# Two attention blocks with expert layers: the exponential of a quad in three instructions, and the second block's normalisation moments and gathers in another order

## The chip, the cores and the metric

The kernel runs on one core of one Trainium2 chip. The metric is the device time of one execution in microseconds. Three runs of the kernel before gave 1275.87, 1277.16 and 1281.9 us, median 1277.16 us.

## What is computed

16 sequences of 112 tokens, model width 256, go through two layers. Each layer adds a cross attention and then a sparse feed-forward part to the residual x:

```
x = x + L0_xcond(layernorm(x), ctx, ctx, tau, delta)      # 16 heads of 16, 375 keys
x = x + L0_ffn(layernorm(x))                              # 64 experts, 8 chosen, and a shared one
x = x + L1_xcond(layernorm(x), ctx, ctx, tau, delta)
x = x + L1_ffn(layernorm(x))                              # 8 experts, 2 chosen

scores = einsum('blhe,bshe->bhls', q, k) * tau + delta
a      = softmax(scores / 4)
out    = einsum('bhls,bshd->blhd', a, v) @ Wo.T + bo
```

All of it is in float32.

## The kernel before, in words

Each engine has its own program, and semaphores couple them. Work falls into four stages: first attention, first experts, second attention, second experts. The change is in the attention stages (the function `attention(L)` of each engine), and what it does to the first attention and to the second differs.

**A batch and its steps.** The attention of a layer runs over 16 batches b (n counts them through both layers, so the second layer's are n = 16 to 31). A batch has NQ = 4 steps i, one for each quad of four heads. In a step TensorE (PE) does, in this order: `scores_T` (L671), the transposed scores of the quad, into PSUM banks 4 to 7, one bank a head, 3 x 112 = 336 columns each; `score_rows` (L653) of the quad that comes three steps later, into banks 0 to 3; the step's jobs; `pv` (L689), exponentials times values, into bank 0; and `max_T` (L661), the transpose of the row maxima. ScalarE (ACT) takes the exponential of banks 4 to 7 (`exp`, L1618) in two instructions of two banks each (672 columns), then evacuates the jobs' results, then `pv`'s (L1631) and `max_T`'s (L1625). VectorE (DVE) takes the row maxima in two instructions of two banks (`row_max`, L1073, "MAX"). `pv` waits for both exponentials and for the first maximum, `max_T` for the second.

**Jobs.** Tables written out by hand name for each step its jobs as (name, batch offset, bank): `FULL` for most batches, `SECOND_FULL` for batch 1 of the second layer, `OPENING_FULL` for batch 0, `CLOSING_FULL` for the last. Jobs are projections and transposes for neighbouring batches: OT and O2T (transposes of the attention output of the batch before, L604 and L585), OP (output projection, L590), XT (transpose of the normalised input of a later batch), Q, K0, K1, V0 to V2 (L590), XT2 and LG (for the router), RK (ranks of the chosen experts, L636). A job in banks 4 to 7 may only start when the exponential has read the bank: banks 4 and 5 wait for the first exponential of the step, 6 and 7 for the second (the line `prev = ...` in `body` of PE). Within a step PE executes in order, so a waiting job holds all that follows. `FIRST_JOBS` lists the work ahead of batch 0; its `FILL` entry issues that many matmuls whose result nobody reads.

**DVE.** `WORK` lists for each step what DVE does between and behind the two maxima. In the second layer: OT; C0 to C3, the sums of eight gathered expert rows into the residual of batch b+3 (`combine`, L1059); MOM, the moments of that residual (`moments`, L1048 and L1052), behind C2 and C3 in step 2 (so ahead of step 3's maxima); OP, MOM2 and LN2 (L1097), which add the attention output, take its moments and normalise it for the router of batch b-1; RK, SLOT, R0 to R3, W80 and W81, the routing. LN2 waits for the factor that POOL works out.

**POOL.** `body1` is the second layer's batch on GpSimd (POOL). In order: scatters of routed rows (L1943), `output_row_numbers` (L1949), gather 0; behind step 1's scores gathers 1 to 3 (L1957, an indirect DMA each) and `deviation(1)` (L1899, L1901), the factor that LN2 waits for; behind step 2's scores gathers 4 and 5, `copy_rows` (L1931, L1932) and `deviation(0)` of batch b+3, which waits for MOM; behind step 3's scores `apply` (L1913), the normalised input that job XT needs, gathers 6 and 7, `add_bias` (L1889). `first()` is the same ahead of batch 0: the gathers of batches 0 to 3, with `normalise(0, base + 2, 2)` between the fourth and the fifth gather of batch 3, then three `add_bias`.

**SyncE** moves queries, keys and transposed maxima in SBUF in its own order (`stream`); the change doesn't touch it, nor any DMA of ACT.

Of the kernel before, what the change touches and what calls it, by code (L numbers as in the profile page):

```python
# [17 lines left out]
ACT = mybir.ActivationFunctionType  # L18
# [3 lines left out]
B, Q, S, D = 16, 112, 375, 256  # L22
KD = D // P
NH, DH = 16, 16
ST, KT = 3, 125
TB = Q * B
EPS = 1e-5
QUAD = 4
NQ = NH // QUAD
# [59 lines left out]
def build(nc, a, acc):  # L89
# [12 lines left out]
    with ctx:  # L102
# [108 lines left out]
        act = sb("act", [P, EM])  # L211
# [117 lines left out]
        def quarters(i):  # L329
# [19 lines left out]
                (("K0", 2, 5), ("RK", -2, 4), ("XT2", -1, 6)),  # L349
                (("K1", 2, 4), ("LG", -1, 5)))  # L350
        OPENING_FULL = ((("K0", 2, 5),), (("Q", 2, 5),), (("K1", 2, 5),), ()), ((("K0", 2, 5),), (("K1", 2, 5),), (("XT", 2, 5),), (("Q", 2, 5),))
        SECOND_FULL = ((("OT", -1, 4), ("V2", 1, 5), ("V0", 1, 7)),
                       (("O2T", -1, 4), ("XT", 2, 5), ("OP", -1, 6), ("V1", 1, 7)),
                       (("K0", 2, 5), ("Q", 2, 4), ("XT2", -1, 6)),
# [11 lines left out]
        TABLE_BANK = 0, 3  # L366

# [32 lines left out]
        def in_layer(b, offset):  # L400

            return not isinstance(b, int) or 0 <= b + offset < B
# [175 lines left out]
        def _(pe):  # L578
# [14 lines left out]
            def attention(L):  # L593
# [81 lines left out]
                def pv(n, u, i, rows_ahead):  # L675

                    g = n * NQ + i
                    pe.wait_ge(s_exp, g * 2 + 2)
                    if rows_ahead:
                        pe.wait_ge(s_max, g * 2 + (2 * AHEAD + 1))  # L680
                    else:
                        pe.wait_ge(s_oev, g)
                    if i == 0:
                        for j in ("V0", "V1", "V2"):
                            pe.wait_ge(ev[j], n + 1)
                    for t in range(ST):
                        for j in range(QUAD):
                            h = QUAD * i + j
                            last = pe.matmul(bank[OUT_BANK][ROW * j:ROW * j + DV, 0:Q], vv[:, u, t, h * DV:(h + 1) * DV],  # L689
                                             pT[:, i % 2 * QUAD + j, t * Q:(t + 1) * Q], start=(t == 0), stop=(t == ST - 1), tile_position=(0, ROW * j))  # L690
                    last.then_inc(s_pv, 1)
# [43 lines left out]
                def body(n, b, u):  # L735
# [9 lines left out]
                    for i in range(NQ):  # L745
# [5 lines left out]
                        for j, r, k in jobs_of(l, b)[i]:  # L751
                            prev = closing.get(k, (s_max, n * (2 * NQ) + 2 * NQ)) if k < 4 else (s_exp, n * (2 * NQ) + (2 * i + (1 if k < 6 else 2)))
# [242 lines left out]
        def _(dve):  # L995
# [69 lines left out]
            def attention(L):  # L1065
# [131 lines left out]
                else:  # L1197
                    WORK = ((("OT", -1), ("MAX", 0), ("C0", 3), ("C1", 3)),
# [408 lines left out]
        def _(act):  # L1607
            def attention(L):
# [3 lines left out]
                def exp(n, i, p):  # L1612

                    g = n * NQ + i
                    act.wait_ge(s_st, g + 1)
                    wait(act, s_pv, g - 1)
                    slot, first_bank = i % 2 * QUAD + 2 * p, ROWS_T + 2 * p
                    act.activation(pT[:, slot:slot + 2, :], banks[0:KT, first_bank:first_bank + 2, 0:ST * Q], ACT.Exp, scale=0.25).then_inc(s_exp, 1)  # L1618
# [109 lines left out]
                def body(n, b, u):  # L1728
                    for i in range(NQ):
                        if i == 2 and (in_layer(b, 3) or l == 0):  # L1730
                            load_ctx((b + 3) % B, 1 - u)
                        exp(n, i, 0)
                        exp(n, i, 1)
# [145 lines left out]
        def _(pool):  # L1879
# [79 lines left out]
            def attention(L):  # L1959
# [3 lines left out]
                def first():  # L1963
                    if l:
# [10 lines left out]
                        gather(3, 1, 0, 4)  # L1975
                        normalise(0, base + 2, 2)
                        gather(3, 1, 4, 4)
# [37 lines left out]
                def body1(n, b):  # L2015
# [14 lines left out]
                    if in_layer(b, -1):  # L2030
                        copy_rows(L, n - 1, b - 1)
                    if in_layer(b, 3):
                        deviation(0, n + 3)
# [3 lines left out]
                    if in_layer(b, 4):  # L2037
                        gather(b + 4, b % 2, 6, 2)
# [161 lines left out]
```

## Time and profile before

| what | value |
|---|---|
| median of three runs | 1277.16 us |
| the profiled execution's own time | 1275.19 us |
| its span, first to last instruction | 1273.3 us |
| busy: PE, DVE, ACT, POOL | 93%, 66%, 40%, 42% |
| mean granted TensorE clock | 0.969 of full |
| first attention, first scores at | 35.07 us |
| second attention, from about 640 us to about | 992 us |

Busy shares are means over four stages with different limits. Start times below are microseconds from the first instruction. In a timeline a row can stand for several instructions of one kind that follow each other (x2 is two); what stands in square brackets is the idle time of the engine just ahead of it, and what ended that. The ends of matmuls are modelled, and consecutive ones overlap. Two instructions of one engine can overlap too: the two exponentials of 0.73 us stand in the timeline as x2 with 1.35 us.

### The profile page before, as it was taken

To read this page: it belongs to the slowest core of one execution; us is meant where nothing else is said; L and a number is where in the kernel's file an instruction comes from. 1 tells how busy PE (TensorE), PEld (TensorE's weight loads), DVE (VectorE), ACT (ScalarE), POOL (GpSimd) and SP (SyncE) were. 2 spreads that over 40 slices of the span, in tenths; PEclk is the share of its full clock that TensorE was granted. 3 is DMA by queue.
4 is the path that set the end of the run, shared out by engine and by line. 5 is a ranking of instruction groups with operands and counts; after the bars stand their busy time and mean duration, and the time that the engine had idled before them with its cause. 6 is when DMAs were issued, how large, how long until landed. Compare 5 with 4: busy or idle time off the path is not lost.

```text
span 1273.3 us, 38557 instructions
## 1 busy us (share of the span) xinstructions
PE 1178.8 (93%) x12856; PEld 929.5 (73%) x12857; DVE 836.6 (66%) x2657; ACT 512.0 (40%) x1289; POOL 535.7 (42%) x691
## 2 busy tenths in 40 slices
PE   6899999998888999999888999998998999999996
PEld 3566666666657999899545666666666899999995
DVE  3468888887876677666555788888875554444442
ACT  2455555555532444444134555555554122222221
POOL 2036666665572001100557667676622223222332
PEclk9899999999998999999977999999997999999998
DMA  4235454546536678865223333333315123353311
GB/s 127 91 126 169 153 167 141 176 148 194 157 102 206 196 217 260 264 179 174 85 80 96 91 110 100 105 103 106 93 49 210 47 39 107 103 168 107 104 33 29
DMA packets 115809, 165.79 MB, mean 130 GB/s; under 512 B 26448, under 2 KB 96736, under 8 KB 114640
## 3 DMA queue, kind: packets, MB, share of 16 engines
q0 software_dynamic: 22672, 58.41, 17.1%
q1 hardware_dynamic: 46464, 53.43, 13.9%
q10 hardware_dynamic: 46528, 52.06, 12.8%
q8 instruction: 86, 1.41, 0.5%
q14 instruction: 59, 0.48, 0.1%
HBM read 85.99 MB, written 61.66 MB: 116 GB/s over the span
## 4 chain that ended last, share of the span: by engine, by line
PE 49%; DVE 9%; issue 6%; POOL 5%; ACT 2%; DMA 1%; DVEq 0%; POOLq 0%; SPq 0%; ACTq 0%
PE banks L945 12%; PE banks L879 9%; PE banks L953 6%; PE banks L590 6%; PE banks L887 4%; PE banks L867 3%; PE banks L671 3%; POOL kept L1957 2%; PE banks L689 2%; DVE mx L1073 2%; DVE resid L1059 2%; ACT shared_buf L1618 1%; POOL xs_d L1943 1%; DVE st L1048 1%; PE banks L661 1%
## 5 line engine op out<-in xcount | busy, mean ns | idle before, releaser
L1073 DVE TENSOR_REDUCE mx<-banks 112x2 f32<-112x750 f32 x256 | 230.8, 933 | 82.3 <-PE banks L653 75.5
L1618 ACT ACTIVATE shared_buf<-banks 125x672 f32<-125x672 f32 x256 | 173.1, 728 | 90.3 <-PE banks L671 86.9
L1943 POOL DMA_INDIRECT xs_d<-xns,idx x160 | 154.3, 964 | 115.5 <-issue 50.2
L1957 POOL DMA_INDIRECT kept<-y_d,yidx x128 | 124.5, 973 | 100.8 <-issue 81.7
L945 PEld LDWEIGHTS banks<-xT,attn_buf 128*128 128x128 f32 x1364 | 157.1, 192 | 1.6
L945 PE MATMUL banks<-xT,attn_buf 128*128 128x128 f32 x1364 | 157.3, 275 | 0.0
L879 PE MATMUL banks<-xT,staged 128*128 128x128 f32 x1064 | 143.5, 278 | 4.6 <-DVE staged L1486 3.8
L879 PEld LDWEIGHTS banks<-xT,staged 128*128 128x128 f32 x1064 | 130.9, 194 | 7.8 <-issue 5.5
L2117 POOL DMA_INDIRECT out<-shared_buf,ids x31 | 53.7, 1733 | 170.1 <-ACT shared_buf L1845 125.9
L590 PE MATMUL banks<-attn_buf,wk 128*128 128x375 f32 x256 | 103.0, 526 | 23.8 <-ACT shared_buf L1618 13.1
L671 PE MATMUL banks<-attn_buf 18*125 18x112 f32 x3072 | 121.5, 288 | 1.1 <-issue 0.5
L671 PEld LDWEIGHTS banks<-attn_buf 18*125 18x125 f32 x3072 | 98.8, 188 | 27.9 <-issue 27.1
L653 PE MATMUL banks<-attn_buf 17*112 17x375 f32 x1024 | 110.1, 498 | 1.7 <-issue 1.7
L689 PE MATMUL banks<-shared_buf,vv 125*17 125x112 f32 x3072 | 102.1, 267 | 8.6 <-DVE mx L1073 8.4
L590 PEld LDWEIGHTS banks<-attn_buf,wk 128*128 128x128 f32 x256 | 45.9, 199 | 78.7 <-ACT shared_buf L1618 48.6
L590 PE MATMUL banks<-wv,attn_buf 128*125 128x256 f32 x384 | 101.9, 391 | 0.7 <-ACT qT L1654 0.7
L689 PEld LDWEIGHTS banks<-shared_buf,vv 125*17 125x17 f32 x3072 | 68.9, 99 | 39.7 <-issue 30.9
L953 PE MATMUL banks<-ringbuf,shared_buf 128*128 x372 | 85.4, 379 | 0.0
L1792 ACT ACTIVATE sgate<-banks 128x128 f32<-128x128 f32 x133 | 36.9, 278 | 113.8 <-PE banks L879 113.8
L1475 DVE COPY xT<-banks 128x256 f32<-128x256 f32 x166 | 70.1, 423 | 16.2 <-DVE yidx_all L1449 7.0
L887 PE MATMUL banks<-ringbuf,shared_buf 128*128 x264 | 79.3, 382 | 0.0
L590 PEld LDWEIGHTS banks<-wv,attn_buf 128*125 128x125 f32 x384 | 69.3, 193 | 12.7 <-issue 2.9
(221 smaller groups left out, 1902.9 us busy)
## 6 DMA issues: line engine op xcount, KB each, us to landing
shared_buf<-xs_d SPq DMA_DIRECT2D x136, 128.0 KB, 2.8
y_d<-shared_buf ACTq DMA_DIRECT2D x132, 128.0 KB, 2.8
ringbuf<-in_we SPq DMA_DIRECT2D x6, 2176.0 KB, 8.8
ringbuf<-in_we POOLq DMA_DIRECT2D x32, 384.0 KB, 4.7
attn_buf<-attn_buf SPq DMA_DIRECT2D x128, 93.8 KB
attn_buf<-in_ctxT ACTq DMA_DIRECT2D x29, 375.0 KB
y_d<-zrow ACTq DMA_DIRECT2D x16, 512.0 KB
xs_d<-zrow ACTq DMA_DIRECT2D x16, 512.0 KB
```

What stands on the lines that cost most here:

```text
L590: last = pe.matmul(dst, lhs(k), rhs(k), start=(k == 0), stop=(k == KD - 1))
L653: last = pe.matmul(bank[j][0:Q, 0:S], qT4[rows, u, i, :], kT4[rows, u, i, :], start=True, stop=True, tile_position=(ROW * j, 0))
L671: last = pe.matmul(bank[ROWS_T + j][0:KT, t * Q:(t + 1) * Q], kT4[rows, u, i, t * KT:(t + 1) * KT], qT4[rows, u, i, :], start=True, stop=T ...
L689: last = pe.matmul(bank[OUT_BANK][ROW * j:ROW * j + DV, 0:Q], vv[:, u, t, h * DV:(h + 1) * DV], pT[:, i % 2 * QUAD + j, t * Q:(t + 1) * Q] ...
L879: last = pe.matmul(bank[u % 2][:, j * P:(j + 1) * P], staged0[:, u % 2, (k * 2 + j) * P:(k * 2 + j + 1) * P], xT[:, u % 2, k, :], start=(k ...
L887: pe.matmul(bank[6 + u % 2][:, 0:D], hT[:, u % 2, 0:P], ringbuf[:, bass.ds(col + 2 * L.up, D)], start=True, stop=True).then_inc(s_dn[0], 1)
L945: last = pe.matmul(dst, weights[:, k * 2 * L.I + c * P:k * 2 * L.I + (c + 1) * P], xT[:, u % 2, k, :], start=(k == 0), stop=(k == KD - 1))
L953: last = pe.matmul(bank[7][:, 0:D], hT[:, u % 2, c * P:(c + 1) * P], ringbuf[:, bass.ds(col + 2 * L.up + c * D, D)], start=(c == 0), stop= ...
L1073: dve.tensor_reduce(mx[:, i % 2, 2 * p:2 * p + 2], banks[0:Q, 2 * p:2 * p + 2, 0:S], AX.X, ALU.max).then_inc(s_max, 1)
L1618: act.activation(pT[:, slot:slot + 2, :], banks[0:KT, first_bank:first_bank + 2, 0:ST * Q], ACT.Exp, scale=0.25).then_inc(s_exp, 1)
L1943: pool.indirect_dma_start(xs_d[L.number], bass.IndirectOffsetOnAxis(ap=idx[:, b % 2, k:k + 1], axis=0), rows, None).then_inc(s_scat[b % 2] ...
L1957: pool.indirect_dma_start(yg[:, u, k, :], None, y_d, bass.IndirectOffsetOnAxis(ap=yidx[:, u, k:k + 1], axis=0)).then_inc(s_gat[u][k * 4 // ...
```

## The change

The exponential of a quad is now taken in three instructions: bank 4 alone, bank 5 alone, banks 6 and 7 together. A job waits for as many of them as cover its bank. Where a step's first job was in bank 5 it is now in bank 4. In the second layer MOM goes from the end of step 2 to behind both maxima of step 3. POOL's gathers 6 and 7 go from behind `apply` to ahead of `deviation(0)`, and ahead of batch 0 all eight gathers of batch 3 go ahead of `normalise`. `FILL` in the second layer's `FIRST_JOBS` is 8 in place of 4.

```diff
-                      (("XT", 0, 0), ("Q", 0, 1), ("DOWN3", 0, 4), ("V2", 1, 4), ("BO", 0, 7), ("ROW0", 0, 0), ("V0", 1, 5), ("FILL", 4, 4), ("MAX0", 0, 6), ("ROW1", 0, 0),
+                      (("XT", 0, 0), ("Q", 0, 1), ("DOWN3", 0, 4), ("V2", 1, 4), ("BO", 0, 7), ("ROW0", 0, 0), ("V0", 1, 5), ("FILL", 8, 4), ("MAX0", 0, 6), ("ROW1", 0, 0),
...
         FULL = ((("OT", -1, 4), ("V2", 1, 5), ("XT", 2, 6), ("V0", 1, 7)),
                 (("O2T", -1, 4), ("Q", 2, 5), ("OP", -1, 6), ("V1", 1, 7)),
-                (("K0", 2, 5), ("RK", -2, 4), ("XT2", -1, 6)),
+                (("K0", 2, 4), ("RK", -2, 5), ("XT2", -1, 6)),
                 (("K1", 2, 4), ("LG", -1, 5)))
-        OPENING_FULL = ((("K0", 2, 5),), (("Q", 2, 5),), (("K1", 2, 5),), ()), ((("K0", 2, 5),), (("K1", 2, 5),), (("XT", 2, 5),), (("Q", 2, 5),))
+        OPENING_FULL = ((("K0", 2, 4),), (("Q", 2, 4),), (("K1", 2, 4),), ()), ((("K0", 2, 4),), (("K1", 2, 4),), (("XT", 2, 4),), (("Q", 2, 4),))
         SECOND_FULL = ((("OT", -1, 4), ("V2", 1, 5), ("V0", 1, 7)),
                        (("O2T", -1, 4), ("XT", 2, 5), ("OP", -1, 6), ("V1", 1, 7)),
-                       (("K0", 2, 5), ("Q", 2, 4), ("XT2", -1, 6)),
+                       (("K0", 2, 4), ("Q", 2, 5), ("XT2", -1, 6)),
                        (("K1", 2, 4), ("LG", -1, 5)))
...
+        EXP_BANKS = (0, 1), (1, 2), (2, QUAD)
+        EXPS = len(EXP_BANKS)
+
+        def exps_behind(k):
+
+            return next(p + 1 for p, (first, end) in enumerate(EXP_BANKS) if k - ROWS_T < end)
...
-                    pe.wait_ge(s_exp, g * 2 + 2)
+                    pe.wait_ge(s_exp, g * EXPS + EXPS)
...
-                            prev = closing.get(k, (s_max, n * (2 * NQ) + 2 * NQ)) if k < 4 else (s_exp, n * (2 * NQ) + (2 * i + (1 if k < 6 else 2)))
+                            prev = closing.get(k, (s_max, n * (2 * NQ) + 2 * NQ)) if k < 4 else (s_exp, n * (EXPS * NQ) + (EXPS * i + exps_behind(k)))
...
-                            (("MAX", 0), ("RK", -2), ("C2", 3), ("C3", 3), ("MOM", 3)),
-                            (("MAX", 0), ("SLOT", -2), ("R3", -2), ("W80", -2), ("W81", -2), ("R0", -1)))
+                            (("MAX", 0), ("RK", -2), ("C2", 3), ("C3", 3)),
+                            (("MAX", 0), ("MOM", 3), ("SLOT", -2), ("R3", -2), ("W80", -2), ("W81", -2), ("R0", -1)))
...
-                    slot, first_bank = i % 2 * QUAD + 2 * p, ROWS_T + 2 * p
-                    act.activation(pT[:, slot:slot + 2, :], banks[0:KT, first_bank:first_bank + 2, 0:ST * Q], ACT.Exp, scale=0.25).then_inc(s_exp, 1)
+                    first, end = EXP_BANKS[p]
+                    slot = i % 2 * QUAD
+                    act.activation(pT[:, slot + first:slot + end, :], banks[0:KT, ROWS_T + first:ROWS_T + end, 0:ST * Q], ACT.Exp, scale=0.25).then_inc(s_exp, 1)
...
-                        exp(n, i, 0)
-                        exp(n, i, 1)
+                        for p in range(EXPS):
+                            exp(n, i, p)
...
-                        gather(3, 1, 0, 4)
+                        gather(3, 1)
                         normalise(0, base + 2, 2)
-                        gather(3, 1, 4, 4)
...
+                    if in_layer(b, 4):
+                        gather(b + 4, b % 2, 6, 2)
                     if in_layer(b, 3):
                         deviation(0, n + 3)
                     after_scores(n, 3)
                     if in_layer(b, 3):
                         apply(0, n + 3, b + 3)
-                    if in_layer(b, 4):
-                        gather(b + 4, b % 2, 6, 2)
```

## Rows read from the trace of the kernel before

**Rows 1.** Windows, one batch of each attention: window, its length, busy us and count by engine, clock, DMA.
```profile
113.39:133.36 19.97, 19.11 (x283) 13.47 (x283) 16.83 (x68) 11.05 (x28) 13.34 (x17) 1.00 0.53 166
...
764.34:785.22 20.88, 19.28 (x284) 13.44 (x283) 17.15 (x49) 11.22 (x29) 14.65 (x21) 1.00 0.35 101
```

**Rows 2.** Waits by engine and line: us in total, times, longest.
```profile
PE banks L590 <- ACT shared_buf L1618: 13.5, 55, 1.7
...
PE banks L604 <- ACT shared_buf L1618: 10.9, 28, 0.8
```

**Rows 3.** Timeline, first attention, steps 0 and 1 of batch 4: start, us, engine, line, what.
```profile
116.97 0.93 DVE L1073 TENSOR_REDUCE mx<-banks 112x2 f32<-112x750 f32 x1
...
118.26 0.36 PE L661 MATMUL banks<-con,mx 112*4 112x112 f32 x2
...
119.54 1.35 ACT L1618 ACTIVATE shared_buf<-banks 125x672 f32<-125x672 f32 x2 [0.63 <-PE banks L671]
...
120.28 1.78 DVE L1073 TENSOR_REDUCE mx<-banks 112x2 f32<-112x750 f32 x2 [0.30 <-PE banks L653]
...
120.32 0.41 PE L585 MATMUL banks<-con,o 112*128 112x112 f32 x2 [0.22 <-ACT shared_buf L1618]
...
120.78 0.36 ACT L1644 ACTIVATE o2T<-banks 128x224 f32<-128x224 f32 x1
...
122.53 0.42 DVE L1089 TENSOR_TENSOR resid<-banks,resid 112x256 f32<-112x256 f32 x1 [0.47 <-PE banks L590]
```

**Rows 4.** Groups by line and form, ACT: busy us, mean ns of one, idle before.
```profile
L1618 ACT ACTIVATE shared_buf<-banks 125x672 f32<-125x672 f32 x256 | 173.1, 728 | 90.3 <-PE banks L671 86.9 <-issue 3.4
...
L1665 ACT ACTIVATE vv<-banks 125x256 f32<-125x256 f32 x96 | 37.0, 385 | 88.3 <-PE banks L590 87.2 <-issue 1.0
```

**Rows 5.** Timeline, DVE, second attention, batches 19 to 21.
```profile
747.92 2.14 DVE L1059 SCALAR_TENSOR_TENSOR resid<-kept,w,resid 112x256 f32<-112x256 f32 x4
...
756.41 0.41 DVE L1097 TENSOR_SCALAR xn<-resid,mv,rstd 112x256 f32<-112x256 f32 x1 [0.62 <-POOL rstd L1901]
...
758.98 2.35 DVE L1059 SCALAR_TENSOR_TENSOR resid<-kept,w,resid 112x256 f32<-112x256 f32 x4
...
762.07 0.18 DVE L1052 BATCH_NORM_AGGREGATE mv<-st 112x2 f32<-112x6 f32 x1 [0.17 <-DVE st L1048]
762.21 1.78 DVE L1073 TENSOR_REDUCE mx<-banks 112x2 f32<-112x750 f32 x2
...
777.27 0.41 DVE L1097 TENSOR_SCALAR xn<-resid,mv,rstd 112x256 f32<-112x256 f32 x1 [0.61 <-POOL rstd L1901]
```

**Rows 6.** Timeline, POOL, second attention, batches 19 and 20.
```profile
762.44 0.21 POOL L1899 TENSOR_SCALAR veps<-mv 112x1 f32<-112x1 f32 x1 [2.66 <-DVE mv L1052]
...
763.43 1.24 POOL L1913 TENSOR_SCALAR xn<-resid,mv,rstd 112x256 f32<-112x256 f32 x1
...
767.18 0.73 POOL L1889 TENSOR_TENSOR resid<-resid,bo 112x256 f32<-112x256 f32 x1
```

**Rows 7.** Timeline, POOL, DVE and PE, opening of the second attention, to batch 17.
```profile
662.12 0.23 POOL L1899 TENSOR_SCALAR veps<-mv 112x1 f32<-112x1 f32 x1 [8.83 <-DVE mv L1052]
...
669.52 2.10 POOL L1889 TENSOR_TENSOR resid<-resid,bo 112x256 f32<-112x256 f32 x3
...
692.33 0.41 DVE L1097 TENSOR_SCALAR xn<-resid,mv,rstd 112x256 f32<-112x256 f32 x1 [7.28 <-POOL rstd L1901]
...
692.88 0.60 PE L585 MATMUL banks<-con,xn 112*128 112x112 f32 x2 [3.38 <-DVE xn L1097]
```

**Rows 8.** Windows of the opening (columns as in rows 1; the clock is third from the end).
```profile
640.00:675.00 35.00, 30.38 (x312) 17.86 (x310) 20.70 (x35) 13.21 (x29) 20.05 (x25) 0.66 0.30 83
675.00:705.00 30.00, 24.73 (x304) 16.69 (x297) 15.75 (x29) 12.70 (x29) 22.56 (x30) 0.83 0.36 99
```

**Rows 9.** Timeline, PE, where the opening's filling matmuls stand.
```profile
639.12 1.05 PE L696 MATMUL banks<-con 128*128 128x128 f32 x8
641.29 0.35 PE L661 MATMUL banks<-con,mx 112*4 112x112 f32 x2 [1.11 <-DVE mx L1073]
```

## The prediction

> **What bounds the kernel now.** Only the two attention stages are touched, so I first took the windows of one batch in each [rows 1]. In the first attention a batch lasts 19.97 us and PE is busy for 19.11 of it, in the second 20.88 with 19.28 busy. PE leads, but the second stage's batch is 0.9 longer for the same PE work, so there another loop sets the pace. Next the waits by line [rows 2]: PE waits for the exponential in nearly every step, 83 times in two rows alone, 24.4 us together. The timeline of a step shows that wait [rows 3]: the exponentials start at 119.54, the first is over 0.73 later, the step's first job starts at 120.32 behind 0.22 us of idle. DVE has little air either. In the same batch its only waits for PE are 0.30 (rows of scores) and 0.47 (OP), so its own chain needs 19.97 - 0.77 = 19.2 us a batch.
>
> In the second attention DVE waits 0.62 for POOL's factor ahead of LN2 [rows 5], and POOL waits 2.66 for DVE's moments [rows 6]. This closes a loop. From LN2's start at 756.41 to the end of MOM at 762.25 is 5.84 us, from there to the next LN2 at 777.27 is 15.02, together 20.86: the batch's 20.88. **This loop, not PE, sets the second attention's batch.** Last the opening: in batch 17 LN2 waits 7.28 and PE 3.38 for it [rows 7], and the clock stands at 0.66 and 0.83 of full in its two windows [rows 8].
>
> **Three exponentials.** No row has 336 columns. ACT's two nearest forms are 256 columns at 385 ns and 672 at 728 [rows 4], 0.82 ns a column, so I take 0.45 us (bounds 0.385 and 0.57, halfway to the larger form). Two exponentials overlap by 2 x 0.73 - 1.35 = 0.11, so three end after 0.45 + 0.45 + 0.73 - 0.22 = 1.41 in place of 1.35. Bank 4 is free 0.28 earlier, bank 5 0.07 later, banks 6 and 7 0.06 later. Every step's first job is now in bank 4 and is longer than the 0.34 until the next bank comes (the shortest, L585, shows 0.41), so the later banks wait for nobody. ACT's 128 extra instructions add 8 us to an engine 40% busy; what they delay is the evacuation queued behind them. That bites once: O2T's evacuation begins when the exponentials end (120.78) and OP needs it, so step 1 gains about 0.1 instead of what the others gain, 0.22 to 0.28 (I take 0.27). On PE alone that makes 3 x 0.27 + 0.1 = 0.9 a batch.
>
> In the first attention DVE doesn't give all of it. The tight cycle is OP, then DVE's chain to the second maximum of the next step 0, then `max_T`, then OP. That maximum ends at 117.90 and `max_T` starts at 118.26 [rows 3]; with some 0.15 for the hand-over 0.2 of slack is left. The cycle shortens by that and by step 1's 0.1: 0.3 a batch, 19.65. Over 14 batches 4.3, with the first and last batch 5.5. Bounds: 2 where the slack is less, and 14 (0.9 x 16) where DVE yields. I stay near the low one, as DVE's own 19.2 stands in the rows.
>
> **MOM behind the maxima, gathers ahead of `deviation(0)`** (second attention). The loop from LN2 to MOM now holds step 3's two maxima, 1.78 [rows 5]: 5.84 + 1.78 = 7.6. From MOM to LN2 two gathers leave POOL's path: `apply` ends at 764.67, `add_bias` starts at 767.18, so 2.51 less a 0.17 hand-over, 2.3. What is left is 12.7. The new period is 20.3, 0.57 less. The gathers go where POOL waited 2.66 [rows 6]; their 2.5 us end about when MOM ended before, and MOM now ends 1.8 later, so they are hidden with 1.5 to spare. Behind MOM wait only DVE's small routing steps (same total, same end) and POOL's `apply`, whose user, XT, comes late in the next step 0 and may wait 0.1 to 0.2 us, ahead of a wait of PE for DVE of about that size. PE's own loop of 20.88 - 1.6 (its idle) - 0.2 and DVE's of 17.15 busy plus gaps stay below 20.3. Batches 19 to 27 hold all of this: 9 x 0.57 = 5.1. Batches 18 and 28 to 31 have fewer gathers and lean on PE; I give them 2.0 together, and batches 16 and 17 0.5 from the exponentials. The bounds of this part are 2 and 12 (0.9 x 14).
>
> **All gathers of batch 3 ahead of `normalise`.** POOL waited 8.83 us at 662.12 for the moments, and the four gathers take 5.0 (two took 2.51 above), so they fit inside. `add_bias`, at 669.52 before [rows 7], starts 5.0 earlier and with it everything up to the factor for batch 17's LN2: that comes about 5 us earlier, against a wait of PE of 3.38. So the whole wait goes; next late is nothing, as K0 and Q occupy PE until about then. The clock follows. The mean of 0.83 over 30 us is 10.2 us at 1.2 GHz [rows 8], behind a gap of 3.38; about 2 of them are the gap's end, the other 8 cost half, 4. Together 7.3. Bounds: 4.0, if the clock falls all the same, and 8.
>
> **FILL 8.** Eight matmul instructions, four of FILL's, take 1.05 us and are followed by 1.11 us of idle [rows 9]; four more fill just that gap, cost 0 (0.1 if they overrun). Over the 35 us from 640 on the clock averaged 0.66, which is 24 us at the lower level [rows 8], and this gap is the first in them. With it filled I expect the clock to hold for about the first half of those 24. That spares at most half of 12 us, of which DVE's sums behind step 0's maxima take back a third: 4. Bounds 0 and 6; the second half has a gap of its own (DVE's moments between two maxima of batch 16), which stays.
>
> **Sum**, against the profiled execution's 1275.2: 5.5 + 5.1 + 2.0 + 0.5 + 7.3 + 4 = 24.4, so 1250.8. The median of the runs shown is 2.0 above that execution; I give half of it, **1252 us**.
>
> **Rivals.** (A) *The clock falls as before in the opening*, FILL or not: then 4 of the 24 are lost, 1256; and if it falls in batch 17 too, 1260. For: the clock doesn't follow the sum of the gaps, since a batch of the second attention has 1.6 us of idle and keeps 1.00 [rows 1]. Against: the largest gap ahead of each is removed.
>
> (B) *PE's 0.9 comes through in full*: DVE's chain in the first attention packs tighter once the rows come earlier. 1252 - 8.5 = 1243. For: DVE is busy for only 16.83 of 19.97 us. Against: the rest is hand-overs inside dependent chains, which no earlier row shortens.
>
> (C) *POOL and DVE block one another.* Four sums of DVE with two SBUF inputs take 2.14 us in step 0 and 2.35 beside POOL's copies [rows 5]. MOM's move puts POOL's `apply`, 1.24 us, beside DVE's two-input routing steps instead of beside the maxima, which read PSUM. If one held the other for its whole length the loop would be 20.3 + 1.24 = 21.5, 0.66 above the 20.88 of before: 5.9 lost in place of 5.1 gained, 1263. The Trainium skill's page "SBUF — State Buffer", section "Who interferes with whom", states this rule: two SBUF inputs on VectorE and a GpSimd instruction that reads SBUF exclude each other for a whole instruction. The trace agrees only that something of the kind exists and prices it at 0.2 for four sums, not 1.24.
>
> (D) *Slower*: PE's many short waits become one. In the new loop PE runs ahead and meets DVE at step 0's `max_T`, with a wait of 0.8 to 1.3 us in each of the batches 19 to 27. If that makes the clock fall as the opening's gap of 1.11 did, each batch runs partly at 1.2 GHz: PE's 19 us with 10 at half is +5, less the 1.3 of idle it eats, so about 3.7 over the 20.3, and 9 x 3.7 = 33, less the 24: 1284. It decides from three batches in four on. Against: the batch in rows 1 keeps 1.00 with 1.6 us of idle in all.
>
> (E) *The earlier bank frees nobody*, because the weight load ahead of the job costs what the wait cost: 5.5 + 2.5 less, 1260.
>
> **Chances.** My forecast 0.43, A 0.20, B 0.13, C 0.06, E 0.11, D 0.03, 0.04 for something unforeseen near no change. The range takes in B with the FILL bound and A and E together: 1242 to 1264. Half a percent, 6.4 us, is about what a measurement of this kernel can tell from no change: faster 0.93, within it 0.04, slower 0.03.
>
> **What the profile after would show.** Right: three exponentials in about 1.41, the first job of a step with no wait for ACT; first-attention batches of 19.6 to 19.7 with DVE's waits for PE shrunk; second-attention batches of 20.3 with POOL's wait for DVE's moments about 1.5; batch 17 without the gap of 3.4 and at full clock; the clock of 640 to 660 at 1.00. Wrong: a wait of PE for L1618 of still 0.2, a LN2 wait in batch 17 above 3 us, or new falls of the clock in batches 19 to 27.

## The result and the profile after

| | before | after |
|---|---|---|
| median of four runs each, same chip | 1277.91 us | 1261.22 us (1254.16 to 1264.85) |
| profiled execution | 1275.19 us | 1254.16 us |
| its span | 1273.3 us | 1252.3 us |
| first attention, from the first scores of batch 0 to those of batch 15's last step | 316.27 | 312.30 |
| second attention, the same | 338.71 | 323.27 |
| the rest of the span | 618.3 | 616.7 |
| time at 1.2 GHz, up to 1240 us | 71.7 | 41.0 |

The ratio is 0.9868, 95% interval 0.984 to 0.9897: 16.7 us faster, with 1252 forecast and a range of 1242 to 1264. The profiled execution of after is the fastest of its four: its mean granted clock is 0.980, that of the others 0.971 to 0.974. So the trace shows 21 us of gain where the medians show 16.7. Here and below a median is over all runs of a kernel, while a ratio leaves out the few that were more than 1.5% slower than the kernel's fastest.

Of the trace's 21 us, 15.4 came in the second attention, 4.0 in the first and 1.6 outside. The windows of the changed kernel: two batches of the first attention, one of the second (from LN2 to LN2), and the opening's two windows (columns as in rows 1).
```profile
149.70:169.31 19.61, 19.26 (x283) 13.49 (x282) 16.86 (x66) 11.41 (x32) 13.32 (x17) 1.00 0.51 155
129.55:149.70 20.15, 19.36 (x283) 13.53 (x283) 16.86 (x66) 11.40 (x32) 13.31 (x17) 1.00 0.52 163
801.00:821.45 20.45, 19.70 (x284) 13.37 (x283) 17.23 (x48) 11.68 (x33) 14.78 (x21) 1.00 0.44 111
640.00:675.00 35.00, 30.11 (x377) 18.59 (x375) 23.59 (x40) 17.37 (x43) 26.30 (x33) 0.80 0.43 108
675.00:705.00 30.00, 29.81 (x427) 20.92 (x427) 22.69 (x51) 16.97 (x48) 22.57 (x31) 1.00 0.41 108
```
In the first attention there are now two kinds of batch, 19.61 and 20.15 us. The 19.97 of [rows 1] was one of the shortest before: batches 2 to 11, where the clock stands at full in both kernels, took 19.97 to 20.44 us, 20.20 in the mean, and take 19.88 now. The second attention's is 20.45 in place of 20.88. Between 675 and 705 us PE is busy for 29.81 of 30 us at full clock, where [rows 8] had 24.73 at 0.83.

The three exponentials stand as foreseen (timeline, first attention, step 2): 1.42 us together, and the job starts 0.50 after their start, with no idle time of PE ahead of it, where [rows 3] had 0.78 and 0.22 of idle.
```profile
302.39 1.42 ACT L1625 ACTIVATE shared_buf<-banks 125x336 f32<-125x336 f32 x3 [0.63 <-PE banks L677]
...
302.89 1.22 PE L596 MATMUL banks<-attn_buf,wk 128*128 128x375 f32 x3
```
Where the gain stands shows in the lengths of a batch's four steps, from `scores_T` to `scores_T`: 5.16, 5.61, 4.75 and 4.45 us before (batch 4), 5.14, 5.55, 4.75 and 4.17 after (batch 6). Only step 3 keeps its 0.28. In step 0 `max_T` now starts 0.84 behind `pv` in place of 0.59, since DVE's second maximum isn't there, and in step 2 the gain is lost ahead of the next `scores_T` (0.28 of idle). From OP to the next step 0's `max_T` it is 16.51 us in place of 16.76, from there to OP 3.10 in place of 3.21.

**The first attention lost one wait and found another.** PE's waits between 34 and 380 us (us in total, times, longest), first before:
```profile
PE banks L590 <- ACT shared_buf L1618: 7.7, 28, 1.7
PE banks L604 <- ACT shared_buf L1618: 5.2, 14, 0.8
...
PE banks L585 <- ACT shared_buf L1618: 1.7, 8, 0.2
...
PE banks L653 <- issue: 1.0, 5, 0.3
```
and after (L659 is `score_rows`, L677 `scores_T`, L596 the projections; L1625 the exponential):
```profile
PE banks L659 <- issue: 5.1, 9, 1.0
PE banks L677 <- issue: 3.3, 11, 0.5
...
PE banks L667 <- DVE mx L1079: 1.9, 4, 0.9
...
PE banks L596 <- ACT shared_buf L1625: 1.4, 1, 1.4
```
13.2 of the 14.6 us of waiting for the exponential went; 4.1 came back ahead of `score_rows`, and 2.8 ahead of `scores_T` (0.5 before, for L671). What `score_rows` waits for shows in SyncE's issues, here at the ends of batches 4 and 5, with PE's rows of scores of step 1 of batches 5 and 6, the first that need these keys (timeline, queue of SyncE, and PE):
```profile
128.36 3.80 SPq L447 DMA_DIRECT2D attn_buf<-qT  x4
132.28 1.18 SPq L442 DMA_DIRECT2D attn_buf<-attn_buf  x2
...
136.11 0.90 PE L659 MATMUL banks<-attn_buf 17*112 17x375 f32 x8 [0.50 <-issue]
...
148.51 2.49 SPq L447 DMA_DIRECT2D attn_buf<-qT  x4
151.11 1.27 SPq L442 DMA_DIRECT2D attn_buf<-attn_buf  x2
...
155.58 0.81 PE L659 MATMUL banks<-attn_buf 17*112 17x375 f32 x8
```
The second half of a batch's key rows (L442) stands on SyncE behind four query rows (L447). Ahead of 6 of the batches 1 to 14 these take 2.5 to 2.9 us to issue; ahead of the other 8 one of the four takes 1.5 to 1.95 in place of 0.6, and the key rows come 1.0 to 1.3 later. Ahead of batches 5 to 11 the query rows took 3.80, 2.49, 3.79, 3.84, 2.49, 2.49 and 3.50 us to issue, and these batches 20.15, 19.61, 20.13, 20.16, 19.61, 19.61 and 20.15: one to one. The earlier four don't follow it all the way (3.80, 3.68, 2.50 and 3.55 go with 19.64, 19.70, 19.69 and 19.96), and batches 12 to 14 are longer in part for other reasons (20.92, 20.44, 21.23). Firmer is the distance: in 8 of the 9 batches with this wait the rows of scores start 2.5 to 2.7 us behind the end of the key rows' issue; in batches without it they start 2.7 to 3.4 behind. The same slow issue stood in the kernel before (timeline, queue of SyncE). There the rows of scores came later and met it by 0.15 to 0.25 us only, five times, also 2.6 to 2.7 us behind the issue:
```profile
131.90 3.79 SPq L441 DMA_DIRECT2D attn_buf<-qT  x4
135.80 1.18 SPq L436 DMA_DIRECT2D attn_buf<-attn_buf  x2
```

**The second attention's loop** (timeline, DVE, POOL and PE):
```profile
801.00 0.41 DVE L1103 TENSOR_SCALAR xn<-resid,mv,rstd 112x256 f32<-112x256 f32 x1
...
808.48 0.22 POOL L1906 TENSOR_SCALAR veps<-mv 112x1 f32<-112x1 f32 x1 [1.58 <-DVE mv L1058]
...
813.57 0.35 PE L667 MATMUL banks<-con,mx 112*4 112x112 f32 x2 [0.65 <-DVE mx L1079]
...
821.45 0.41 DVE L1103 TENSOR_SCALAR xn<-resid,mv,rstd 112x256 f32<-112x256 f32 x1 [0.44 <-POOL rstd L1908]
```
From LN2 to POOL's start behind MOM are 7.5 us, from there to the next LN2 13.0: LN2 still waits for POOL and POOL for MOM, so the same loop still closes, 0.4 shorter. In each of the batches 19 to 26, before and after, LN2 starts 0.25 to 0.27 behind the end of POOL's factor, and POOL waits for MOM, 2.66 before and about 1.57 after. PE's four waits of 0.22 for the exponential and one of 0.74 ahead of step 3's `pv` have become one of 0.65 at `max_T`.

**The last batch of the second attention** gave 3.0 of the 15.4 us, and they go with the clock (windows over the first three steps of batch 31, before and after, columns as in rows 1):
```profile
970.37:988.92 18.55, 16.97 (x186) 12.31 (x185) 7.67 (x35) 5.85 (x14) 3.76 (x7) 0.54 0.87 331
952.37:967.89 15.52, 12.51 (x185) 9.02 (x185) 7.30 (x32) 6.03 (x17) 3.76 (x7) 0.78 0.92 356
```
17.1 us of it were at 1.2 GHz before, 6.8 after.

### The profile page after: what moved, and what is told of

It reads as the page before. It is cut to its first block, busy times and chain, and to the rows that moved or that the text cites. A ratio compares the mean times of both kernels' runs of the same rounds, so it can differ in the third digit from the quotient of the medians.

```text
span 1252.3 us, 38827 instructions
## 1 busy us (share of the span) xinstructions
PE 1172.1 (94%) x12864; PEld 923.9 (74%) x12865; DVE 836.8 (67%) x2657; ACT 521.8 (42%) x1417; POOL 537.6 (43%) x691
## 3 DMA queue, kind: packets, MB, share of 16 engines
q8 instruction: 86, 1.41, 0.5%
## 4 chain that ended last, share of the span: by engine, by line
PE 49%; DVE 14%; issue 7%; POOL 2%; ACT 1%; DMA 1%; DVEq 1%; POOLq 0%; ACTq 0%
PE banks L951 13%; PE banks L885 10%; PE banks L959 6%; PE banks L596 6%; DVE mx L1079 4%; PE banks L893 4%; PE banks L873 3%; PE banks L677 2%; DVE resid L1065 2%; PE banks L659 2%; PE banks L695 1%; POOL kept L1964 1%; DVE st L1054 1%; PE banks L667 1%; DVE eq L1128 1%
## 5 line engine op out<-in xcount | busy, mean ns | idle before, releaser
L1625 ACT ACTIVATE shared_buf<-banks 125x336 f32<-125x336 f32 (+1 forms) x384 | 181.1, 544 | 86.9 <-PE banks L677 83.0
L677 PE MATMUL banks<-attn_buf 18*125 18x112 f32 x3072 | 119.4, 285 | 4.2 <-issue 4.0
L677 PEld LDWEIGHTS banks<-attn_buf 18*125 18x125 f32 x3072 | 97.1, 185 | 30.8 <-issue 30.2
L659 PE MATMUL banks<-attn_buf 17*112 17x375 f32 x1024 | 107.6, 486 | 7.4 <-issue 6.8
L596 PE MATMUL banks<-attn_buf,wk 128*128 128x375 f32 x256 | 100.4, 515 | 10.9 <-DMA wv<-in_wv 9.2
L596 PE MATMUL banks<-wv,attn_buf 128*125 128x256 f32 x384 | 101.1, 389 | 1.3 <-ACT qT L1661 0.7
L596 PEld LDWEIGHTS banks<-attn_buf,wk 128*128 128x128 f32 x256 | 44.7, 194 | 60.6 <-ACT shared_buf L1625 29.5
L1572 DVE TENSOR_TENSOR shared_buf<-sgate,banks 128x512 f32<-128x512 f32 x32 | 22.0, 687 | 85.8 <-ACT sgate L1843 85.8
```

The lines of the kernel that those rows point to most:

```text
L596: last = pe.matmul(dst, lhs(k), rhs(k), start=(k == 0), stop=(k == KD - 1))
L659: last = pe.matmul(bank[j][0:Q, 0:S], qT4[rows, u, i, :], kT4[rows, u, i, :], start=True, stop=True, tile_position=(ROW * j, 0))
L677: last = pe.matmul(bank[ROWS_T + j][0:KT, t * Q:(t + 1) * Q], kT4[rows, u, i, t * KT:(t + 1) * KT], qT4[rows, u, i, :], start=True, stop=T ...
L1625: act.activation(pT[:, slot + first:slot + end, :], banks[0:KT, ROWS_T + first:ROWS_T + end, 0:ST * Q], ACT.Exp, scale=0.25).then_inc(s_ex ...
```

## The experiments

Three groups, each with runs of the kernel before between its own. The first group, on one chip: 34 runs of before, median 1277.46 us, and 11 or 12 of each part of the change. Lengths of batches are of one profiled execution each.

**The three exponentials alone**, with the banks of the jobs:
```diff
+        EXP_BANKS = (0, 1), (1, 2), (2, QUAD)
...
-                (("K0", 2, 5), ("RK", -2, 4), ("XT2", -1, 6)),
+                (("K0", 2, 4), ("RK", -2, 5), ("XT2", -1, 6)),
```


> The three exponentials and the bank numbers alone, all else as before. Theory of loops: the first attention gets 4 us shorter, the second attention's batches 19 to 27 stay at 20.88 because DVE and POOL set them, so 5 to 8 us in all (1270 to 1273). Rival, every wait of PE that is removed comes off the time: 0.22 to 0.28 us in each of 103 steps, 23 to 29 us (1250 to 1255).

1274.79 us, ratio 0.9986 (0.9959 to 1.0012): not to be told from no change, and short of the 5 to 8 us expected. The second attention's batches 19 to 25 stay at 20.65 to 20.91, so that loop doesn't feel the exponentials, and the large gain of the rival is out. Batch 31 does differ: its first three steps take 15.5 us with 6.8 of them at 1.2 GHz, as in the whole change, where before and the three other parts have 16.8 to 18.6 us with 13 to 17. That is one execution each, and why is open. PE's waits in the first attention:
```profile
PE banks L659 <- issue: 5.7, 9, 1.0
PE banks L677 <- issue: 3.0, 10, 0.5
```
The new waits come with this part alone. One of them, 1.03 us at 217.01, stands at the start of a stretch with the clock at 0.57 (window, columns as in rows 1), which the kernel before doesn't have there. That the wait brought the fall isn't shown, as a wait of 0.96 in batch 1 had none behind it:
```profile
217.00:225.00 8.00, 7.99 (x56) 5.51 (x56) 3.69 (x11) 2.10 (x6) 3.56 (x6) 0.57 0.65 207
```

**The order alone** (MOM behind the maxima, gathers ahead of `deviation(0)`):
```diff
-                            (("MAX", 0), ("RK", -2), ("C2", 3), ("C3", 3), ("MOM", 3)),
-                            (("MAX", 0), ("SLOT", -2), ("R3", -2), ("W80", -2), ("W81", -2), ("R0", -1)))
+                            (("MAX", 0), ("RK", -2), ("C2", 3), ("C3", 3)),
+                            (("MAX", 0), ("MOM", 3), ("SLOT", -2), ("R3", -2), ("W80", -2), ("W81", -2), ("R0", -1)))
...
+                    if in_layer(b, 4):
+                        gather(b + 4, b % 2, 6, 2)
                     if in_layer(b, 3):
                         deviation(0, n + 3)
...
-                    if in_layer(b, 4):
-                        gather(b + 4, b % 2, 6, 2)
```


> MOM behind both maxima and gathers 6 and 7 ahead of deviation(0), nothing else. Theory of loops: batches 19 to 27 fall from 20.88 to about 20.35, 5 to 7 us in all (1271 to 1273). Rival, POOL and DVE exclude each other for whole instructions: these batches rise to 21.5, 6 us slower.

1275.02 us, ratio 0.9971 (0.9941 to 1.0001): the time alone tells little, and the 5 to 7 us expected didn't come. Batches 20 to 25 take 20.35 to 20.57 us, without the exponentials and with smaller waits of PE at `max_T`, 0.3 to 0.5 a batch (waits of 770 to 890 us):
```profile
POOL veps L1899 <- DVE mv L1052: 9.4, 6, 1.6
...
PE banks L661 <- DVE mx L1073: 1.9, 5, 0.5
```
LN2 again starts 0.25 to 0.28 behind POOL's factor. So it is the loop through LN2, MOM and POOL that makes the 20.4, not PE's wait of 0.65 in the whole change; and the batches are far from the 21.5 of rival C. What MOM's move and the gathers' move give each wasn't run.

**The gathers of the opening alone**, and **FILL 8 alone**:
```diff
-                        gather(3, 1, 0, 4)
+                        gather(3, 1)
                         normalise(0, base + 2, 2)
-                        gather(3, 1, 4, 4)
```


> Only batch 3's eight gathers ahead of normalise, before batch 0 of the second attention. Theory: the gap of 3.4 us in batch 17 goes and the fall of the clock behind it, batch 17 from 28.1 to about 21, 6 to 8 us in all (1270 to 1272). Rival, the clock falls somewhere else instead: 3.5 us.

1270.03 us, ratio 0.9953 (0.9924 to 0.9983), as expected.
```diff
-                      (("XT", 0, 0), ("Q", 0, 1), ("DOWN3", 0, 4), ("V2", 1, 4), ("BO", 0, 7), ("ROW0", 0, 0), ("V0", 1, 5), ("FILL", 4, 4), ("MAX0", 0, 6), ("ROW1", 0, 0),
+                      (("XT", 0, 0), ("Q", 0, 1), ("DOWN3", 0, 4), ("V2", 1, 4), ("BO", 0, 7), ("ROW0", 0, 0), ("V0", 1, 5), ("FILL", 8, 4), ("MAX0", 0, 6), ("ROW1", 0, 0),
```


> Only FILL 8 in place of 4. Theory of the prediction: the clock holds for the first half of the opening, 4 us (1274). Rival, where the clock falls depends on more than this gap, and it falls a few us later all the same: 0 to 2 us, which a measurement can't tell from none.

1273.3 us, ratio 0.9973 (0.9947 to 0.9999), near the 4 us expected. The opening's windows, with the gathers moved:
```profile
640.00:675.00 35.00, 30.36 (x278) 18.02 (x279) 20.04 (x34) 12.17 (x26) 23.46 (x29) 0.68 0.32 92
675.00:705.00 30.00, 28.53 (x374) 20.16 (x377) 20.75 (x39) 14.43 (x37) 21.43 (x28) 0.86 0.35 97
```
and with FILL 8:
```profile
640.00:675.00 35.00, 28.89 (x318) 18.73 (x320) 23.31 (x41) 12.92 (x29) 22.47 (x29) 0.89 0.34 96
675.00:705.00 30.00, 26.61 (x295) 18.17 (x288) 16.30 (x31) 11.67 (x28) 23.13 (x30) 0.73 0.34 93
```
The gathers take batch 17 from 28.13 to 22.93 us: the gap goes, and the clock doesn't fall at 691 us any more, but it stays low from 666 to 684 (17.1 us, where before had 10.2). FILL takes batch 16 from 24.12 to 21.37 and batch 17 from 28.13 to 29.18. In the whole change they take 22.59 and 19.91: together 9.8 us less than before, where the two edits alone add up to 6.9.

**What belongs to the clock.** The four medians are 2.7, 2.4, 7.4 and 4.2 us below before, together 16.7, the whole change's gain. That they meet is partly chance: by the means the four are together 12.7 below. The runs of one kernel spread by nine to twenty us, and with the mean granted clock. Over the 81 runs of this group, within each kernel, 0.01 of mean clock goes with 7.4 us (standard error 0.4), and only 1.7 us of scatter is left. With that slope the mean of each part splits:

| part | mean clock (before 0.969) | mean against before | of it with the clock | at equal clock |
|---|---|---|---|---|
| exponentials | 0.962 | -1.4 | +5.5 | -6.9 |
| order | 0.967 | -2.2 | +2.0 | -4.1 |
| opening's gathers | 0.972 | -6.2 | -2.0 | -4.2 |
| FILL 8 | 0.973 | -2.9 | -2.5 | -0.4 |

The last column has a standard error of 0.6. It is a regression over runs, not an edit that holds the clock still; but it fits the traces: FILL works through the clock alone, and the exponentials give back in clock most of what they gain. Where they lose it is seen in one execution only: 20.5 us at 1.2 GHz in the first attention, where before had 6.8, and so has the whole change.

The second group, on another chip where the same kernel takes 8.5% longer (17 runs of before, median 1386.29 us, and 6 of each kernel, 12 of the third). First the change again, and without its FILL:

> The changed kernel once more, to see how far its time moves from execution to execution and with what. If the clock's falls are what differs: the batches keep their 19.6 to 20.5 us, and the time follows the number of us at 1.2 GHz (each about half a us), 1254 to 1265.

1370.58 us, ratio 0.9889 (0.982 to 0.9957). The range expected was the first chip's.

> The changed kernel with FILL 4, as before. Theory of the prediction, the filling keeps the clock up ahead of batch 0: 4 us slower than the changed kernel. Rival, the other parts have moved the falls anyway: within 1 us of it.

1364.62 us, ratio 0.9883 (0.9822 to 0.9945). Within the whole change FILL makes no difference that these runs can tell. Then MOM between the two maxima of step 3:
```diff
-                            (("MAX", 0), ("MOM", 3), ("SLOT", -2), ("R3", -2), ("W80", -2), ("W81", -2), ("R0", -1)))
+                            (("MOM", 3), ("MAX", 0), ("SLOT", -2), ("R3", -2), ("W80", -2), ("W81", -2), ("R0", -1)))
```


> The changed kernel with MOM between the two maxima of step 3 instead of behind both. Theory of the loop of DVE and POOL: 0.93 us less in the loop, so batches 19 to 27 fall from 20.42 to where the cycle through OP and max_T holds them, 19.9 to 20.0, 4 us in all. Rival, the wait of PE for the second maximum in step 0 (0.65 us) is what sets the batch, not the loop: no change, or slower by the 0.8 that the second maximum of step 3 comes later.

1368.83 us, ratio 0.991 (0.9875 to 0.9945): the same as the change. And delta loaded by ACT behind the last exponential of step 3, not by SyncE:
```diff
-                        load_delta((b + 2) % B, u)
...
                         for p in range(EXPS):
                             exp(n, i, p)
+                        if i == NQ - 1 and (in_layer(b, 2) or l == 0):
+                            act.dma_start(kT4[ONE:P:ROW, u].rearrange("p i s -> p (i s)"), a["delta"][bass.ds((b + 2) % B, 1), :].rearrange("o s -> (o s)").partition_broadcast(QUAD)).then_inc(s_delta[u], 16)
```


> The changed kernel with the load of the additive row issued by ACT behind the exponentials of step 3 instead of by SP ahead of the key rows. Theory: in the first attention PE's new stop ahead of step 1's score rows is the wait for the key rows' transfer, queued on SP; with 0.6 us less in that queue step 1 is 5.55 us in every batch instead of 6.1 in half of them, 3 us in all. Rival, the stop comes from something else: no change.

1367.73 us, ratio 0.9898 (0.9843 to 0.9953): no difference either. But neither of the last two got a real test, as the traces show: on this chip other waits set the batches. The exponentials, DVE's maxima and the evacuations stand, mostly 1.7 to 3 us at a time, for something that the trace calls remote, which is to say that it found no releaser on this core, though the matmuls that they read have ended by the record (changed kernel on this chip: waits over the span, and one in the timeline, 1.8 us behind the end of `pv`):
```profile
DVE mx L1079 <- remote: 50.0, 19, 11.4
...
ACT shared_buf L1625 <- remote: 25.0, 8, 8.4
```
```profile
831.92 0.77 PE L695 MATMUL banks<-shared_buf,vv 125*17 125x112 f32 x24
...
834.48 0.26 ACT L1638 ACTIVATE oT<-banks 128x112 f32<-128x112 f32 x1 [2.07 <-remote]
```
The first chip's traces have no such wait. Here the first attention's batches take 21.4 us and more from batch 4 on, the second's 21.7 to 25.7 between batches 18 and 27, and the wait ahead of step 1's rows of scores appears twice in place of nine times. What the remote wait is stays open.

The third group asks for the share of the exponentials in the whole and for a version that beats the change. It ran on a third chip, which behaves like the second (11 runs of before, median 1393.37 us, and 6 of each kernel). The second kernel is the change with two exponentials a quad and the banks of before.

> The changed kernel as it is, as the measure for the next three. Clock theory (the profiled execution of the change was a lucky one): the median is 15 to 18 us below before, and the profiled execution lies within 5 us of its own median. In the first attention the batches come in two kinds, 19.6 us and 20.1 us, and the longer kind is the one whose step 1 waits 0.3 to 0.5 us ahead of its rows of scores. Rival (the 20.1 are chance or clock): the two kinds don't go with that wait.

1370.65 us, ratio 0.9803 (0.9747 to 0.9858). Both numbers of the clock theory missed: the median is 22.7 us below before, and the profiled execution, at 1386.06 with a clock of 0.923, lies 15.4 above it.

> The whole change without its first part: two exponentials a quad and the banks of before; order, opening gathers and FILL 8 as in the change. Theory (the first part is worth 0.2 to 0.3 us a batch in the first attention and nothing in the second, whose batch is set by DVE and POOL): 3 us slower than the change, first attention 316 us from first to last batch in place of 312, second attention's batches 20.4 as with the change. Rival 1 (the exponentials carry more once the loop is looser): 7 to 10 us slower, second attention's batches 20.7 or more. Rival 2 (worth nothing): within 1 us of the change.

1374.65 us, ratio 0.9879 (0.984 to 0.9918).

> The change, with the load of delta issued by ACT behind the last exponential of step 3 and not by SP ahead of the key rows. Theory (in the changed kernel step 1's rows of scores wait for the key rows' transfer, which stands on SP's queue behind delta, 0.51 us, and the query rows): the key rows are issued 0.5 us earlier, the wait of 0.3 to 0.5 us in step 1 goes, the first attention's 20.1 us batches become 19.6, which with 8 such batches is 4 us. Rival (DVE's chain takes over at once): the wait goes but step 2 or step 0 grows by as much, 0 to 1 us.

1370.33 us, ratio 0.982 (0.977 to 0.9871). The fourth adds to it, in the second attention:
```diff
-                    WORK = ((("OT", -1), ("MAX", 0), ("C0", 3), ("C1", 3)),
+                    WORK = ((("MAX", 0), ("OT", -1), ("C0", 3), ("C1", 3)),
...
-                            (("MAX", 0), ("MOM", 3), ("SLOT", -2), ("R3", -2), ("W80", -2), ("W81", -2), ("R0", -1)))
+                            (("MOM", 3), ("MAX", 0), ("SLOT", -2), ("R3", -2), ("W80", -2), ("W81", -2), ("R0", -1)))
```


> The change, delta by ACT, and in the second attention DVE takes MOM between the two maxima behind step 3, and OT behind the second maximum behind step 0. Theory (the second attention's loop runs over LN2, MOM and POOL, and PE's only long wait there is 0.65 us at the first row of maxima of step 0): MOM 0.9 us earlier, so batches of 19 to 27 at 19.9 to 20.1 in place of 20.4, 3 to 4 us, and with delta's 4 us 7 us faster than the change. Rival (MOM in between makes step 3's second maximum 0.6 late, which takes the place of what it gave): batches stay at 20.4, no faster than c3.

1363.61 us, ratio 0.9784 (0.9732 to 0.9836).

What the exponentials are worth within the whole stays unsettled. The medians say 4.0 us, the ratios, 0.9803 against 0.9879, 10.6, and the split by clock (here 9.7 us for 0.01) 5.1 with a standard error of 2.3: more than nothing, but neither the theory's 3 nor the rival's 7 to 10 is excluded. Delta by ACT is again nothing that can be told. The last kernel has the lowest time of the group, 7.0 below the change by the medians, 2.6 by the ratios and 4.0 at equal clock (standard error 2.3). Its interval overlaps the change's, so it is a candidate and not a faster kernel. None of the expected batch lengths could be read: the profiled change has batches of 21.4 us and longer in the first attention from batch 4 on, and 22.4 to 27.9 for batches 18 to 29.

## Why the prediction was right, and where not

**The size is right, and it is no sum of right terms.** The predicted 24.4 us against the profiled execution meets 21.0 in the profile and 16.7 in the medians. By place, from the two traces:

| term | predicted | in the trace |
|---|---|---|
| first attention | 5.5 | 4.0 |
| batches 16 and 17 (exponentials, gathers, FILL) | 0.5 + 7.3 + 4 | 9.8 |
| batches 19 to 27 | 5.1 | 1.5 |
| batches 18 and 28 to 31 | 2.0 | 4.1 |
| all else | 0 | 1.6 |

In the last row but one 3.0 us are batch 31 and the clock, which no term foresaw: luck. And the fast profiled execution flatters the 1252: the median is 9 us above it.

**Exponentials: the mechanism right, SyncE and the clock left out.** 1.41 us for three is 1.42, PE's wait is gone, and a clean first-attention batch takes 19.61 us for 19.65 predicted. The tight cycle gave what it was said to give: 0.25 from OP to `max_T` for a slack of 0.2, 0.11 from there to OP for 0.1. Over batches 2 to 11 the mean fell by 0.32 for 0.3. At equal clock the part is worth 6.9 us for 5.5 and 0.5 predicted. The step that failed is that its price was named in durations only: tighter batches ran into the key rows (4.1 us of waits more than before), and alone the mean clock was 0.007 lower, 5.5 us. Of the change's steps I followed those of PE, ACT and DVE, and never asked whether SyncE's transfers would be there when PE came 0.3 earlier.

**Rival E is out**, as the earlier bank did free PE; so is B, 0.9 a batch: PE's busy time in a batch rose from 19.11 to 19.26 and the 19.61 leave no more. D's wait at `max_T` appeared as its mechanism said, but smaller, 0.65 in place of 0.8 to 1.3: eight times between 705 and 860 us, 5.4 us together, and no stretch at 1.2 GHz lies between 668 and 878 us. In batch 27 the clock did fall, below; the prediction had named that as a sign of being wrong.

**The order: 20.3 predicted, 20.42 measured, and then two bad batches.** The loop's halves were 7.6 and 12.7, and are 7.5 and 13.0. POOL's wait for MOM of 1.5 is 1.58. But the term of 5.1 for batches 19 to 27 came to 1.5: 3.4 from batches 19 to 25, and 1.9 lost in 26 and 27. There, POOL and DVE (timeline, changed kernel), with PE:
```profile
856.07 0.95 POOL L1950 DMA_INDIRECT xs_d<-xns,idx  x1 [2.13 <-issue]
...
864.01 0.41 DVE L1103 TENSOR_SCALAR xn<-resid,mv,rstd 112x256 f32<-112x256 f32 x1 [1.90 <-POOL rstd L1908]
...
864.57 0.38 PE L591 MATMUL banks<-con,xn 112*128 112x112 f32 x2 [0.86 <-DVE xn L1103]
865.42 0.77 PE L695 MATMUL banks<-shared_buf,vv 125*17 125x112 f32 x24 [0.46 <-DVE mx L1079]
875.96 0.77 PE L695 MATMUL banks<-shared_buf,vv 125*17 125x112 f32 x24 [0.83 <-issue]
877.38 0.35 PE L667 MATMUL banks<-con,mx 112*4 112x112 f32 x2 [0.65 <-DVE mx L1079]
```
In batch 26 the second scatter is held back 2.13 us where 0.30 is usual, and the batch is 1.65 longer than its neighbours. The same scatter of the kernel before (timeline, POOL) was held back 0.94:
```profile
874.43 0.94 POOL L1943 DMA_INDIRECT xs_d<-xns,idx  x1 [0.94 <-issue]
```
0.64 more than usual, and that batch was 0.62 longer: in both kernels a stall of POOL lengthens the batch by nearly its own length, which is the best sign that POOL is in the loop. With the order alone it is 2.13 too, with 21.81 and 23.08 us for the two batches. At the start of batch 27 something else follows (timeline, DVE and POOL, changed kernel; above a usual batch, below this one):
```profile
810.62 0.23 DVE L1176 TENSOR_SCALAR sc<-logits,wsum 112x8 f32<-112x8 f32 x1
810.89 0.73 POOL L1896 TENSOR_TENSOR resid<-resid,bo 112x256 f32<-112x256 f32 x1 [0.18 <-POOL xn L1920]
...
873.90 0.76 DVE L1176 TENSOR_SCALAR sc<-logits,wsum 112x8 f32<-112x8 f32 x1
873.90 0.72 POOL L1896 TENSOR_TENSOR resid<-resid,bo 112x256 f32<-112x256 f32 x1 [0.18 <-POOL xn L1920]
```
A routing step of DVE starts together with POOL's `add_bias` and lasts as long as it, 0.76 for 0.23. Another, beside `apply`, takes 0.41 for 0.23. With the order alone both are there too, 0.76 and 0.42. Counted from POOL's start behind MOM, DVE's first maximum of step 0 comes 0.79 later than in the usual batch, and PE's waits of 0.83 and 0.65 stand behind it. The clock falls from 879 to 882, which makes batch 27 22.18 us. The prediction took a steady loop; why the new order makes the scatter's stall longer stays open. The 2.0 for batches 18 and 28 to 31 came to 1.1 in batch 18, nothing in 28 to 30 and the 3.0 of the clock in batch 31.

**The opening's gathers: 7.3 predicted, 7.4 by the medians, 6.2 by the means.** The 8.83 of waiting did hold the four gathers; the factor comes in time for PE, and LN2's wait for it went from 7.28 to 2.87. In the whole change batches 16 and 17 went from 52.25 to 42.50 us, 9.8 less. The clock part, 4 by the prediction, came in the profile of the whole change (0.83 to 1.00) and only in small part with this edit alone (0.86).

**FILL: the mechanism right, its size within the whole not settled.** The 1.11 of idle at `max_T` is 0.22. The clock in 640 to 675 is 0.80 for 0.66, not the 1.00 that I named for the first 20 us; it falls from 646, behind the next waits (timeline, PE, changed kernel):
```profile
637.18 0.35 PE L667 MATMUL banks<-con,mx 112*4 112x112 f32 x2 [0.22 <-DVE mx L1079]
...
643.77 0.35 PE L667 MATMUL banks<-con,mx 112*4 112x112 f32 x2 [1.05 <-DVE mx L1079]
...
655.68 0.35 PE L667 MATMUL banks<-con,mx 112*4 112x112 f32 x2 [1.77 <-DVE mx L1079]
```
Between 640 and 660 it is 0.84. Alone FILL gave 4.2 by the medians (2.9 by the means) for 4 predicted; taken out of the whole on another chip it cost nothing that could be seen.

**Rival A** is half true: in the profiled execution batches 16 and 17 have 13.7 us at 1.2 GHz in place of 27.6, and the whole 41.0 in place of 71.7; in the other three runs the mean clock shows more of it, 0.006 to 0.009, which by the slope above is 4 to 7 us, most of the distance from the profiled 1254 to the median 1261. **Rival C is out as a price on every batch**: they are at 20.4 and not at 21.5, POOL's `apply` beside DVE's routing steps takes 1.24 us as it did beside the maxima [rows 6], and DVE is busy for 17.23 us in the batch where it was for 17.15. The rule on shared access (the Trainium skill, "SBUF — State Buffer", "Who interferes with whom") fits the trace in part: the two-input routing step that runs beside `apply` (L1128) takes 0.33 for 0.23 and doesn't wait for `apply`'s end 0.7 later, while in batch 27 a step of DVE was held for the whole length of POOL's `add_bias`.

## What to carry to other kernels

Where an edit lets one engine run ahead, list every producer that it will meet next, the DMA queue of an idle-looking engine too, and look for its slowest instance in the trace, not its usual one: a stall that is hidden today is the next wait. In a loop of dependent engines a stall of one engine comes through nearly whole, 0.64 as 0.62 before and 1.83 as 1.65 after, so a period read from the usual batch is a lower bound. And where runs spread with the granted clock, time each part over many runs and set the clock against the time, since a part can gain 7 us at equal clock and show 1.

## What the runs showed of the hardware that was not expected

The mean granted clock goes with most of the spread of one kernel on one chip: 34 runs of the kernel before lie between 1269.06 us (clock 0.978) and 1284.54, correlation -0.92. One part of the change shifted this mean by itself, from 0.969 to 0.962 with the exponentials.

The same kernel took 1277, 1386 and 1393 us on three chips, with clocks of 0.969, 0.935 and 0.930 on average. By the slopes found within a chip, 7 to 11 us for 0.01, the clock accounts for a part of that only. Between the profiled executions of the change on the first two chips 94 of 116 us lie in the attention stages, where the waits marked remote stand that the first chip doesn't show; that they are the cause isn't shown. The ratio of the change was nevertheless 0.987, 0.989 and 0.980.

A small instruction of DVE can be held for the length of one of POOL's: 8 columns took 0.76 us in place of 0.23 beside a sum of 256 columns on POOL that took 0.72, in the profiled executions of the change and of the order alone, once each.
